# Folding a butterfly into dense weights: who makes the second scaled copy of each pair of blocks

## The reference, cut to what matters

```python
h = jnp.einsum('bsd,dh->bsh', x, W_exp) + b_exp
h = butterfly(h, up_weights, D_HIDDEN)
h = jax.nn.gelu(h + up_bias, approximate=False)
h = butterfly(h, down_weights, D_HIDDEN)
y = jnp.einsum('bsh,hd->bsd', h, W_con) + b_con
...
na = w[..., 0, 0] * a + w[..., 0, 1] * b
nb2 = w[..., 1, 0] * a + w[..., 1, 1] * b
```

## Time and profile before

| | before |
|---|---|
| median of 3 runs | 4975.23 us (4973.64 to 4977.94) |
| the profiled execution | 4974.19 us, its span 4972.5 us |
| busy share of the span | PE 81%, DVE 54%, ACT 29%, POOL 26% |
| the butterfly stage | 272.8 to 469.4 us of the span |
| VectorE's 32 groups | 313.2 to 373.3 us (matrix 0) and 382.3 to 438.2 us (matrix 1) |

### The profile page before, as it was taken

How to read it: one execution, slowest core, us unless ns; L and a number is a source line. 1 busy time by engine, 2 the same in 40 slices (tenths; PEclk the granted TensorE clock), 3 DMA queues, 4 the chain that set the end, 5 groups by cost and what they waited for, 6 DMA issues and landing times. The chain is left out here.

```text
span 4972.5 us, 63780 instructions
## 1 busy us (share of the span) xinstructions
PE 4046.5 (81%) x20652; PEld 3295.3 (66%) x20652; DVE 2692.0 (54%) x9090; ACT 1435.4 (29%) x2190; POOL 1301.9 (26%) x1123
## 2 busy tenths in 40 slices
PE   6833898756878866678689788695999999999998
PEld 4712777636767765667658666574888787887886
DVE  8644545438988989989535445322443445322222
ACT  2344333235555544455310000121211112111111
POOL 0000000002121120121136414102576775433332
PEclk8666999878888887788899889897999999999999
DMA  1134222260110100100124422334122223100000
GB/s 56 37 117 119 68 83 79 66 193 28 30 42 12 44 26 10 39 30 12 41 92 140 140 73 110 120 127 139 50 71 65 74 74 99 33 26 20 22 25 20
DMA packets 244966, 329.93 MB, mean 66 GB/s; under 512 B 67013, under 2 KB 125253, under 8 KB 242375
## 3 DMA queue, kind: packets, MB, share of 16 engines
q1 hardware_dynamic: 152568, 175.70, 11.9%
q10 hardware_dynamic: 89568, 142.64, 8.5%
q0 software_dynamic: 2560, 8.39, 0.4%
HBM read 217.55 MB, written 109.10 MB: 66 GB/s over the span
## 5 line engine op out<-in xcount | busy, mean ns | idle before, releaser
L1496 PE MATMUL xa_ps_t<-xa_diag,xa_s_buf 128*128 128x128 f32 x4096 | 503.0, 283 | 161.7 <-DVE xa_s_buf L1677 96.8
L1496 PEld LDWEIGHTS xa_ps_t<-xa_diag,xa_s_buf 128*128 128x128 f32 x4096 | 486.9, 198 | 192.0 <-DVE xa_s_buf L1677 114.3
L1625 DVE MAX8 xa_cand<-xa_s_buf 128x8 f32<-128x64 f32 x4096 | 534.9, 217 | 115.6 <-issue 56.9
L2938 DVE CAST m_act_hl<-m_g 128x512 fp32r<-128x512 f32 x256 | 137.7, 538 | 831.9 <-ACT m_g L2806 831.9
L2632 POOL TENSOR_TENSOR m_act_hl<-m_g,m_act_hl 128x512 fp32r<-128x512 f32 x256 | 355.5, 1389 | 660.0 <-DVE m_act_hl L2938 660.0
L2806 ACT ACTIVATE m_g<-m_ps_h,m_b 128x512 f32<-128x512 f32 x256 | 176.1, 688 | 1096.2 <-PE m_ps_h L82 1091.1
L1441 POOL TENSOR_TENSOR xa_aT<-xa_a,xa_aT 128x512 fp32r<-128x512 f32 x128 | 159.7, 1269 | 1006.6 <-ACT xa_a L1561 1006.6
L80 PE MATMUL m_ps_h<-m_hT,m_w 128*128 128x512 f32 x1024 | 413.7, 404 | 6.4 <-issue 4.3
L80 PE MATMUL m_ps_o<-m_w,m_act_hl 128*128 128x512 f32 x1024 | 406.9, 397 | 0.7 <-POOL m_act_hl L2632 0.7
L82 PE MATMUL m_ps_o<-m_w,m_act_hl 128*128 128x512 f32 x1024 | 406.6, 397 | 0.0
L81 PE MATMUL m_ps_o<-m_w,m_act_hl 128*128 128x512 f32 x1024 | 406.5, 397 | 0.0
(11 more groups left out here) (366 smaller groups left out, 8119.5 us busy)
## 6 DMA issues: line engine op xcount, KB each, us to landing
at_xk<-in_x_dram SPq DMA_DIRECT2D x128, 128.0 KB, 2.7
spectrum<-df_yo ACTq DMA_DIRECT2D x32, 512.0 KB, 2.8
id_raw<-spectrum SPq DMA_DIRECT2D x32, 512.0 KB, 3.8
m_xt<-x ACTq DMA_DIRECT2D x64, 256.0 KB, 3.5
ky_raw<-in_ctx_dram SPq DMA_DIRECT2D x16, 768.0 KB, 6.3
xa_ks<-kt SPq DMA_DIRECT2D x48, 256.0 KB
xa_raw<-in_ctx_dram SPq DMA_DIRECT2D x32, 384.0 KB, 3.3
w<-bf_out_t SPq DMA_DIRECT2D x32, 256.0 KB, 2.4
```

The costliest lines, as they stand in the source:

```text
L1496: last = pe.matmul(ps_t[:, c // 4, c % 4, :], s_buf[:, t % 2, h, k0:k0 + P], diag[:, h, :], start=(h == 0 and c % 4 == 0), stop=(h == HEAD ...
L1625: dve.max(out=ranks[h][:, :, g], in_=s_buf[:, t % 2, h, g * SEG:(g + 1) * SEG])
```

## The change: what it does

ScalarE keeps the first copy of each pair, and GpSimd makes the second, with a `tensor_scalar` multiplication of the same block by the other coefficient. The new copy has a semaphore of its own, `s_part2`, and VectorE waits for both counts ahead of each group. GpSimd runs all 64 copies in the order of the pairs, under the same conditions on `s_grp` as ScalarE.

```diff
@@ -521,6 +521,7 @@
+        s_part2 = sem("second_partners_scaled")
@@ -572,6 +573,30 @@
+                def partners(matrix, i, q):
+
+                    s = ORDERS[matrix][i]
+                    x, col, width = (wc, col_dn, D) if matrix == 0 else (wT, col_up, D + 1)
+                    a = block_pairs(s)[q][0]
+                    n = (HC // 2) * (TOP * matrix + i) + q
+                    if i >= 1:
+                        pool.wait_ge(s_grp, GROUPS * (TOP * matrix + i - 1) + group_of(ORDERS[matrix][i - 1], a) + 1)
+                    elif matrix == 1:
+                        pool.wait_ge(s_bias, 1)
+                        pool.wait_ge(s_mmc, HC)
+                    if n >= SLOTS:
+                        pool.wait_ge(s_grp, (n - SLOTS) // 2 + 1)
+                    other = 1 if matrix == 0 else 2
+                    pool.tensor_scalar(part[:, n % SLOTS, 1, 0:width], x[:, a, 0:width], col[:, s, q, other:other + 1], None, ALU.mult)\
+                        .then_inc(s_part2, 1)
+
+                pool.wait_ge(s_wc, 16)
+                pool.wait_ge(s_cols, 16 * 10)
+                for matrix in range(2):
+                    for i in range(TOP):
+                        for q in range(HC // 2):
+                            partners(matrix, i, q)
@@ -643,10 +668,7 @@
-                    other = 1 if matrix == 0 else 2
-                    act.activation(part[:, n % SLOTS, 0, 0:width], x[:, a, 0:width], ACT.Copy, scale=col[:, s, q, 0:1])
-                    act.activation(part[:, n % SLOTS, 1, 0:width], x[:, a, 0:width], ACT.Copy,
-                                   scale=col[:, s, q, other:other + 1]).then_inc(s_part, 1)
+                    act.activation(part[:, n % SLOTS, 0, 0:width], x[:, a, 0:width], ACT.Copy, scale=col[:, s, q, 0:1]).then_inc(s_part, 1)
@@ -723,6 +745,7 @@
                     dve.wait_ge(s_part, n + 2)
+                    dve.wait_ge(s_part2, n + 2)
```

## The result

| | before | after |
|---|---|---|
| median (14 runs of each, side by side) | 4975.22 us (4967.82 to 4980.27) | 4984.32 us (4982.58 to 4990.27) |
| ratio after / before | | 1.0021, 95% interval 1.0013 to 1.0029 |
| the profiled execution, its span | 4974.19 us, 4972.5 us | 4983.31 us, 4981.6 us |
| VectorE's groups, matrix 0 | 60.06 us | 67.15 us |
| VectorE's groups, matrix 1 | 55.89 us | 61.82 us |

The change makes the kernel slower, by 9 us at the median. That it is slower is plain; whether by more than 0.2% is not, since the interval reaches to both sides of that.

What follows compares the result with a forecast made beforehand. VectorE was taken to bound the butterfly stage, waiting at times for ScalarE's copies. Terms +30.0 copies, -11.8 waits, -2.1 starts and +1.6 second semaphore gave +17.7 us on 4974.2: 4992 us, range 4974 to 5020.

Steps and rivals of the forecast that it cites:

- The rival in which the two do not exclude each other: Butterfly stage: GpSimd's copies cost VectorE nothing, c is 0; -11 us, 4963 us; chance 0.10.
- from end to end: Butterfly groups: each GpSimd copy costs VectorE its whole length, c = 0.84 us; +38 us, 5012 us; chance 0.08.
- The length of a copy, p: Duration of GpSimd's second copy at 512 columns: taken as 0.75 us, bounded by 0.52 and 1.27.
- c = p - 0.25: VectorE's cost per GpSimd copy in the groups: the copy's length less the hidden start, 0.50 us.
- Rows: VectorE's groups: 60 copies beside them at 0.50 us each lengthen its work by +30.0 us.
- Idle time: VectorE's waits for ScalarE's copies in both matrices: 11.8 of 12.9 us go.
- the second wait: Second semaphore on VectorE ahead of each of 32 groups: 0.05 us each, +1.6 us.
- Starts: Ahead of group 0 of each matrix: 1.6 us in place of 2.65, together -2.1 us.
- GpSimd as the bound: Rival for the butterfly groups: two GpSimd copies take longer than a group of 3.03 us; no chance of its own.
- a microsecond that VectorE's 32 groups gain or lose is one of the kernel's: End of the butterfly stage: only a barrier and other stages follow, so group time passes whole into kernel time.
- the wash: Rival: exclusion holds but copies are cheap, p 0.52 to 0.65 us; +3 to +11 us, 4978 to 4985; chance 0.24.
- the signs that were named ahead: Expected profile: VectorE rows median 0.75, mean around 1.2 us; groups near 4.1; matrices about 9 and 8 us longer.

Runs made afterwards that it cites:

- the experiment with PSUM: Changed kernel with VectorE's first input read from a cleared PSUM tile instead of block b, bias column left out: 4969.14 us, ratio 0.9988 to before.

## Why the prediction was right or wrong

**The mechanism was right.** The copies are not hidden: VectorE's rows stretch beside GpSimd's, as the earlier trace rows had it, and the experiment with PSUM shows that the second SBUF input is the reason. The rival in which the two do not exclude each other is out. So is "from end to end": a copy of 1.56 us costs VectorE 0.34 us of longer rows (20.5 us over 60 copies), far from its whole length. The rule of the Trainium skill, "SBUF — State Buffer", "SBUF: two separate sides", that they exclude each other for the whole instruction, agrees with these rows in that there is an exclusion, and differs from them in its length.

**The length of a copy, p: wrong.** The prediction took 0.75 us and said "Above: an operation with two inputs takes 1.27 us". The runs show 1.56, which by the prediction's own sign (p from 0.65 to 1.0) makes it wrong in its size. One operation does not bound another of a different kind, however much more that one has to read: here the one-input multiplication takes 1.57, a plain copy 0.61 and a two-input operation 1.04. The 769 ns of the Trainium skill, "GPSIMD Engine Reference", section 3.1, is not the time of this operation either; the trace's 1566 ns decides.

**The cost from the length, c = p - 0.25: wrong for this operation.** With the true p it would have given 1.31 us a copy, and a sum of about 70 us, with the starts as they came out. It holds for the two-input operation (0.80 at 1.04), from which it came. The multiplication costs VectorE 0.34 in rows, 0.41 with the new waits. The two mistakes nearly cancel, since 0.50 was predicted. That they do is luck: with the right length and the same rule the time would have come out at 5044, beyond the range.

**The terms one by one.** Rows: +30.0 predicted, +20.5 measured. Idle time: -11.8 and +1.6 for the second wait, -10.2 together, against -7.4; the waits for ScalarE went as predicted, with two left that came to 1.2 us, and the second wait costs 3.09 - 3.03 = 0.06 for 0.05, but 4.4 us of waits for GpSimd came in, where the prediction had its copies "never late". Starts: -2.1 predicted, +1.3 measured, since two copies of 1.56 take longer than ScalarE's four of 0.72. The stage: +17.7 predicted, +14.4 measured.

**The rival without a chance.** "GpSimd as the bound" was left out because two copies were to take at most 2.54 us against 3.03. They take 3.13. The experiment with PSUM shows GpSimd as the bound once the exclusion is gone. In the changed kernel the two engines wait by turns; had SBUF cost nothing, GpSimd would still have held the groups at 3.1 to 3.2.

**The time.** 4984.3 lies 8 us below the forecast: 3 of them are the stage's terms, and the other 5 are the step "a microsecond that VectorE's 32 groups gain or lose is one of the kernel's", which held for a delay of 31.6 us and is in doubt near 14.5. It lies inside the band of the wash (4978 to 4985), but not for its reason: the copy was not cheap. Of the signs that were named ahead, the stretched and plain rows by turns and the median of 0.75 came true; the mean of a row is 0.90 in place of 1.2, the groups come at 3.71 and 4.12 in place of 4.1 throughout, and the matrices are 7.7 and 6.6 us longer with their starts in place of 9 and 8.

## What to carry to other kernels

A helper engine is not free because it stands idle: what it reads may lie in the way of the engine that sets the pace, and the row lengths of that engine show it. Price an operation from a row of its own kind, or run it by itself in an idle stretch, before a bound from another kind is trusted. Where one engine is late only in some stages, more slots may do, at the price of SBUF alone, what a second engine does at a price in time; here they gave 4 us, where the change lost 9.

## What the runs showed of the hardware

GpSimd's multiplication by one value (1.57 us per partition, 1.49 by a constant, at 128x512) is longer than a `tensor_tensor` with the value repeated (1.04) and yet keeps VectorE out for half as long or less (0.21 to 0.41 us against 0.80). A `tensor_tensor` whose second input is repeated takes 1.04 us where a full one takes 1.27. With eight slots the same multiplication stretched VectorE by 0.21 us a copy, with four by 0.35.
